# Similarity rows by broadcast DMAs from DRAM, and wider modulations on VectorE from batch 4 on, in a gated cross-attention kernel

## What is computed

```python
def xattn(feature, embedding, weight):              # both (16, 128, 1024), weight (128, 128, 3)
    # per column t: cosine similarity of column t with its left neighbour, itself, its right neighbour
    sim = stack([cos(emb, emb_l), cos(emb, emb), cos(emb, emb_r)], axis=1)   # (16, 3, 1024)
    att = repeat(sim, C, axis=1)                    # (16, 384, 1024): rows 0-127 left, 128-255 own, 256-383 right
    inp_unf = stack([f_pad[:, :, k:k + T] for k in range(3)], axis=2).reshape(B, C * 3, T)
    return einsum('bit,oi->bot', inp_unf * att, weight.reshape(O, C * 3))

def ffn(x):                                         # 8 experts of rank 16, the two best of each token
    gates = top2(softmax(x @ router_w.T + router_b)), normalised
    return einsum('ner,eor->no', (x @ A) * gates, Bm) * 0.5

x = x + tanh(g_xattn) * xattn(layernorm(x), ctx, conv_weight)
x = x + tanh(g_ffn) * ffn(layernorm(x))
```

## Time and profile before

| | |
|---|---|
| median of three runs | 235.19 us (232.73 to 235.48) |
| the profiled execution's own time | 237.36 us |
| its span | 234.8 us |
| TensorE (PE) busy | 216.1 us, 92% |
| VectorE (DVE) busy | 164.7 us, 70% |
| ScalarE (ACT) busy | 112.8 us, 48% |
| GpSimd (POOL) busy | 80.8 us, 34% |
| moved by DMA | 27.24 MB |

### The profile page before, as it was taken

One profiled execution on the slowest core, in us unless ns is written; L12 is line 12 of the kernel. 1 busy time (PEld: TensorE's weight loads), 2 busy tenths in 40 slices (PEclk: granted clock), 3 DMA queues, 4 the chain that ended last, 5 costly groups with the idle time before them and its releaser, 6 DMA issues.

```text
span 234.8 us, 3431 instructions
## 1 busy us (share of the span) xinstructions
PE 216.1 (92%) x1056; PEld 125.5 (53%) x1056; DVE 164.7 (70%) x403; ACT 112.8 (48%) x192; POOL 80.8 (34%) x216
## 2 busy tenths in 40 slices
PE   5878978989999999989999999989999999999954
PEld 5542523636564555547464545546565665666632
DVE  1274986395999666495998665595988777786552
ACT  3566967446387456052577464161647172221210
POOL 2340463205076534032175633032234151412430
PEclk9997999999999999999999999999999999999997
DMA  5789600607022625212233202211142202020132
GB/s 210 267 306 347 264 1 22 248 0 250 20 89 101 259 91 215 100 57 77 89 121 112 93 37 92 89 48 74 59 179 91 91 0 89 3 89 33 57 150 118
DMA packets 8880, 27.24 MB, mean 116 GB/s; under 512 B 1632, under 2 KB 2240, under 8 KB 8864
## 3 DMA queue, kind: packets, MB, share of 16 engines
q1 hardware_dynamic: 8432, 26.78, 30.8%
q10 hardware_dynamic: 432, 0.26, 0.4%
HBM read 18.65 MB, written 8.39 MB: 115 GB/s over the span
## 4 chain that ended last, share of the span: by engine, by line
PE 75%; DVE 13%; issue 4%; POOL 2%; ACT 2%; DMA 2%; POOLq 0%; DVEq 0%
PE bank L852 29%; PE bank L877 13%; PE bank L838 8%; PE bank L804 7%; PE bank L866 5%; DVE pt L661 3%; PE bank L895 3%; PE bank L896 3%; PE bank L897 3%; DVE x L668 2%; DMA et<-ctx 2%; PE bank L824 2%; DVE bn L673 1%; PE bank L902 1%; POOL pr L343 1%
## 5 line engine op out<-in xcount | busy, mean ns | idle before, releaser
L852 PE MATMUL bank<-pt,wT 128*128 128x512 f32 x192 | 99.5, 600 | 0.0
L661 DVE TENSOR_TENSOR pt<-xn,bank 128x512 f32<-128x512 f32 x96 | 63.7, 672 | 12.4 <-PE bank L838 7.9
L877 PEld LDWEIGHTS bank<-aT,xT 128*128 128x128 f32 x256 | 34.4, 190 | 11.1 <-issue 10.2
L838 PE MATMUL bank<-rows,sel 96*128 96x512 bf16 x96 | 36.0, 382 | 3.7 <-DVE pt L661 2.3
L852 PEld LDWEIGHTS bank<-pt,wT 128*128 128x128 f32 x192 | 31.0, 190 | 12.9 <-issue 6.0
L877 PE MATMUL bank<-aT,xT 128*128 128x136 f32 x256 | 34.9, 279 | 0.0
L490 ACT ACTIVATE xT<-bank 128x512 f32<-128x512 f32 x32 | 19.1, 595 | 31.3 <-PE bank L866 31.2
L378 POOL CAST topf<-topi 128x2 f32<-128x2 uint32 x16 | 3.0, 186 | 81.7 <-DVE topi L692 81.7
L668 DVE TENSOR_TENSOR x<-bank,xt 128x512 f32<-128x512 f32 x32 | 21.9, 686 | 9.8 <-PE bank L852 9.8
L705 DVE TENSOR_TENSOR x<-bank,x 128x512 f32<-128x512 f32 x32 | 21.7, 679 | 8.3 <-PE bank L897 8.3
L838 PEld LDWEIGHTS bank<-rows,sel 96*128 96x128 bf16 x96 | 9.2, 97 | 32.8 <-DVE pt L661 16.6
(11 more groups left out here) (86 smaller groups left out, 260.6 us busy)
## 6 DMA issues: line engine op xcount, KB each, us to landing
et<-ctx SPq DMA_DIRECT2D x16, 512.0 KB, 5.8
xt<-x SPq DMA_DIRECT2D x16, 512.0 KB, 3.4
out<-x SPq DMA_DIRECT2D x15, 512.0 KB, 2.6
aT_in<-expert_aT SPq DMA_DIRECT2D x1, 544.0 KB, 13.1
bm_in<-expert_b SPq DMA_DIRECT2D x1, 512.0 KB, 12.3
out<-x SPq DMA_DIRECT2D x2, 256.0 KB, 2.0
sel<-select SPq DMA_DIRECT2D x1, 216.0 KB, 13.5
wT_in<-conv_wT SPq DMA_DIRECT2D x1, 192.0 KB, 6.0
```

The lines of the kernel that those rows point to most:

```text
L661: nc.vector.tensor_tensor(pt[:, i, :], xn[:, n % 2, h * HALF + t:(h + 1) * HALF + t], sim_ps[k % 2][:, :], ALU.mult).then_inc(mod_done, 1)
L838: nc.tensor.matmul(sim_ps[k % 2][:, :], sel[:, SLOT_OF[n], t, :], rows[:, q % 2, half(h)], start=True, stop=True).then_inc(spread, 1)
L852: nc.tensor.matmul(conv_ps[h][:, :], wT[:, t * P:(t + 1) * P], pt[:, i, :], start=(t == 0), stop=(t == TAPS - 1)).then_inc(tap_done, 1)
L877: last = nc.tensor.matmul(h_ps[:, 0:ER + E], xT[:, n % 2, c, :], aT[:, c, :], start=(c == 0), stop=(c == KC - 1))
```

## The change

- From batch 4 on (`SPREAD = 4`) TensorE does not spread similarity rows. The similarities stay fp32 (`simf`), four transposes turn them into rows, ACT copies these to SBUF (`rows_out`), SP stores them to a DRAM tensor `simd` and waits for it (`store_rows`), and loads them back as a tile `att` of 128 partitions x 3 taps x 1024 columns (`load_att`), seven DMAs per batch, into one of three buffers: three DMAs of 42 partitions whose source repeats one row of 4 KB, and four short ones for the two channels whose taps fall into two thirds.
- From batch 4 on VectorE modulates 1024 columns at once from SBUF (`modulate_both`), in the odd steps of the batch before. `pt` has two buffers.
- POOL keeps the products of tiles 1 and 2; all others are VectorE's. POOL sums A's eight blocks into one (`sum_means`), so TensorE's means are one matmul.
- The tables of steps move for groups 2 to 4; `normalize` is issued a step earlier; four more warm-up matmuls; the start's loads are reordered: the two gates first on ACT's queue, the three constants to SP's.
- Code that is not run before or after (for `WHOLE` shorter than six steps) is removed.

```diff
-WARM_UP = 7
+WARM_UP = 11
+SPREAD = 4
-NEIGHBOURS = {(0, 4): 1, (2, 3): 2, (6, 3): 3, (10, 3): 4}
-ROWS = {(0, 5): 1, (3, 0): 2, (7, 0): 3, (11, 0): 4}
-ON_POOL = (1, 2, 5, 7, 9, 11, 13, 15)
+NEIGHBOURS = {(0, 4): 1, (2, 0): 2, (6, 0): 3, (10, 0): 4}
+ROWS = {(0, 5): 1, (2, 1): 2, (6, 2): 3, (10, 2): 4}
+ON_POOL = (1, 2)
...
+            def store_rows(q):
+                sp.wait_ge(rowsf_done, q - 1)
+                for z in range(2):
+                    sp.dma_start(simd[GROUPS[q][0]:GROUPS[q][0] + G, :, PAD + z * HALF:PAD + (z + 1) * HALF].rearrange("b f t -> f b t"),
+                                 rowsf[32 * z:32 * z + 2 * G, :]).then_inc(rows_stored, 16)
+
+            def load_att(n):
+                third = [simd[n:n + 1, 0, PAD - 1:PAD - 1 + T], simd[n:n + 1, 1, PAD:PAD + T], simd[n:n + 1, 0, PAD:PAD + T]]
+                full = P // TAPS
+                j = n % 3
+                sp.wait_ge(rows_stored, 16 + 32 * (GROUP_OF[n] - 1))
+                if n - 3 >= SPREAD:
+                    sp.wait_ge(mod_done, modulations(n - 3))
+                for f in range(TAPS):
+                    c = f * (full + 1)
+                    sp.dma_start(att[c:c + full, j, :, :],
+                                 third[f].unsqueeze(1).to_broadcast([full, TAPS, T])).then_inc(att_in[j], 16)
+                for c in (full, 2 * full + 1):
+                    for f in sorted({(TAPS * c + t) // P for t in range(TAPS)}):
+                        taps = [t for t in range(TAPS) if (TAPS * c + t) // P == f]
+                        sp.dma_start(att[c:c + 1, j, taps[0]:taps[-1] + 1, :],
+                                     third[f].unsqueeze(1).to_broadcast([1, len(taps), T])).then_inc(att_in[j], 16)
...
                 for e in {1: (8, 9), 2: (10, 11), 4: (12, 13), 5: (14, 15)}.get(n, ()):
                     load_e(e)
+                if n % 4 == 2 and n + 2 < B:
+                    store_rows(GROUP_OF[n + 2])
+                if SPREAD <= n + 2 < B:
+                    load_att(n + 2)
...
+            def sum_means():
+                pool.wait_ge(aT_in_done, 16)
+                nc.gpsimd.tensor_tensor(aT_sum[:, :, :], aT_in[:, 0:4, :], aT_in[:, 4:8, :], ALU.add).then_inc(summed_means, 1)
...
+            def rows_out(q):
+                act.wait_ge(rowsT_done, q + 1)
+                if q > 2:
+                    act.wait_ge(rows_stored, 16 + 32 * (q - 2))
+                nc.scalar.activation(rowsf[:, :], rows_ps(q)[0:40, :], ACT.Copy).then_inc(rowsf_done, 1)
...
+            def modulate_both(n, t):
+                dve.wait_ge(xn_done, n + 1)
+                dve.wait_ge(att_in[n % 3], 16 * 7 * (len(range(n % 3, n + 1, 3)) - len(range(n % 3, SPREAD, 3))))
+                dve.wait_ge(tap_done, STEPS * (n - 1))
+                nc.vector.tensor_tensor(pt[:, n % 2, t, :], xn[:, n % 2, t:t + T], att[:, n % 3, t, :],
+                                        ALU.mult).then_inc(mod_done, 1)
...
+                    if SPREAD <= n + 1 < B and i % 2 == 1:
+                        modulate_both(n + 1, i // 2)
+                        some(norms, 2)
...
-            act.dma_start(onehot[:, :, :], one_hot).then_inc(onehot_in, 16)
-            act.dma_start(ident[:, :], identity).then_inc(ident_in, 16)
-            act.dma_start(shifts[:, :, :], shift).then_inc(shifts_in, 16)
+            act.dma_start(gates_in[:, 0:1], g_xattn.rearrange("(a n) -> a n", a=1).to_broadcast([P, 1])).then_inc(gates_in_done, 16)
+            act.dma_start(gates_in[:, 1:2], g_ffn.rearrange("(a n) -> a n", a=1).to_broadcast([P, 1])).then_inc(gates_in_done, 16)
```

More of the change, by code:

```diff
@@ L95, in flamingo_kernel @@
         rows = sb("rows", [96, 2, T], BF16)
+        simf = sb("simf", [P, 4, 2, 32])
+        rowsf = sb("rowsf", [40, HALF])
+        nothing = sb("nothing", [B, PAD])
+        att = sb("att", [P, 3, TAPS, T])
+        simd = nc.dram_tensor("simd", (B, 2, PAD + T), F32).ap()
         xt = sb("xt", [P, G, T])
@@ L159, in rows_ps @@
         def rows_ps(q):
[L160 removed]
+            return sum_ps(q)[:, :].bitcast(BF16) if q < 2 else sum_ps(q)[:, :]
         onehot_in = sem("onehot_in")
@@ L200, in flamingo_kernel @@
         rowsT_done = sem("rowsT_done")
+        rowsf_done = sem("rowsf_done")
+        rows_stored = sem("rows_stored")
+        att_in = [sem(f"att_in{j}") for j in range(3)]
         rows_left_done = sem("rows_left_done")
@@ L239, in flamingo_kernel, with modulations @@
         block = st.enter_context(nc.Block())
-        SETUP = 11
+        SETUP = 13
         def half(h):
             return slice(h * HALF, (h + 1) * HALF)
[L245 to L250, removed]
+        def modulations(n):
+            return STEPS * min(n + 1, SPREAD) + TAPS * max(n + 1 - SPREAD, 0)
         def products_up_to(e):
@@ L537, in _ @@
                     m = STEPS * n + i
-                    for q in (ROWS.get((n, i)),):
-                        if q is not None:
-                            rows_left(q)
-                    for k in steps_at(m, modulated):
-                        if not whole(k):
-                            modulated_hi(k)
+                    if (n, i) in ROWS:
+                        q = ROWS[n, i]
+                        rows_left(q) if q < 2 else rows_out(q)
                     if i == 0 and n >= 2:
                         second_weight(n - 2)
-                    if i == 1 and n + 1 < B:
+                    if i == 0 and n + 1 < B:
                         normalize(n + 1)
@@ L821, in transpose_similarities @@
             def transpose_similarities(q):
+                if q >= 2:
+                    pe.wait_ge(sim_done, q + 1)
+                    for w in range(4):
+                        last = nc.tensor.transpose(rows_ps(q)[0:40, w * P:(w + 1) * P],
+                                                   simf[:, w, :, :].rearrange("p z k -> p (z k)")[:, 0:40], ident[:, :])
+                    last.then_inc(rowsT_done, 1)
+                    return
                 pe.wait_ge(split, 5 * (q + 1))
```

125 lines of the change are left out of this document (57 added, 68 removed).

## The result

The changed kernel takes **273.5 us** (median of four runs, 272.76 to 275.76) against 235.09 us for the kernel before in the same session: 1.166 times as long, 95% interval 1.157 to 1.176. The forecast was 221.8 us.

What follows compares the result with a forecast made beforehand. TensorE, busy 92% of the span, was taken as the bound. -15.8 (spreads) - 2.0 (head) - 1.0 (batch 2) + 5.4 (waits) = -13.4 us, from 237.36 to 224.0, or 221.8 from the 235.19 median; range 213 to 239.

Steps and rivals of the forecast that it cites:

- the rate of the load: Loading att from DRAM: taken as fast as the load of x, 370 GB/s, thanks to equally long 4 KB packets.
- the gap in which it was to hide: Batches without the three waits: att lands after 8.7 us, asked for 9.39 us later at the soonest, hidden by 0.7.
- Rival (3): att loads: reading one 4 KB row from all engines runs at half rate, making the kernel slower, 251 us; chance 0.14.
- decision point: Rival (3): 13.4 us are lost at a load some 2.3 us longer, near 240 GB/s.
- The rule of the Trainium skill on 14 engines: att loads: 42 partitions run on 14 engines, thirds take 4.8 instead of 4.2 us, the sum 1.8 us more.
- The spreads, -15.8: TensorE from batch 4 on: 72 spreads of 0.22 us leave the chain, saving 15.8 us; plain batch 9.39.
- VectorE, 0 but for batch 3: VectorE's modulations gain only evenness; plain batch 8.1 us, hidden behind TensorE's 9.39; batch 3 is 1.1 us late.
- The three waits, +5.4: VectorE waits 2.0 us for att at batches 3, 7 and 11; price 2.6, 1.3 and 1.5, 5.4 us given back.
- The head, -2.0: Start: the gate loads come first on ACT's queue, POOL is free 2.3 us earlier; 2.0 us taken as saved.
- the means cost nothing: Start: experts' means go from 16 TensorE passes (1.86 us) to two, VectorE gets product(5); counted as nothing.
- Batch 2, -1.0: Batch 2: splits into bf16 parts and the copy of rows go; 1.0 of 1.33 us idle TensorE saved.
- the sum: The forecast's terms added up: -13.4 us against the profiled execution's 237.36, giving 224.0, or 221.8 by medians.

Runs made afterwards that it cites:

- sixteen: Changed kernel with each batch's att in three loads of 48, 48 and 32 neighbouring partitions and no short loads: 253.61 us, ratio 1.080.
- after: The changed kernel itself, with 42-partition loads and short pieces, against the kernel before: 273.5 us, ratio 1.166.
- no_short: Changed kernel with att in three loads of 42, 42 and 44 neighbouring partitions and no short loads: 268.46 us, ratio 1.140.
- fast_head: Changed kernel with one 128-partition load per batch from 128 context rows, means on TensorE, products 5 and 7 on POOL: 232.41 us, ratio 0.988.
- wide_distinct: Changed kernel with one load of 128 partitions per batch, from 128 different context rows each read for three taps: 238.21 us.
- wide_same: Changed kernel with one load of 128 partitions per batch, from one repeated row: 244.49 us, ratio 1.038.
- distinct: Changed kernel with the large loads reading another context row for every partition and tap instead of one repeated row: 274.63 us, ratio 1.168.
- gates_first: Kernel before with only the start's loads reordered as in the changed kernel: 235.63 us, ratio 1.0015.
- spread32: Changed kernel with att in four loads of 32 partitions, each taking every fourth partition, from one repeated row: 245.42 us, ratio 1.045.
- noload2: Changed kernel loading att only for batches 4, 5 and 6, later batches using old data: 245.49 us, ratio 1.042.
- warm: Changed kernel with means on TensorE and 70 idle matmuls before experts_out in batches 5, 7 and 11: 286.41 us, ratio 1.220.
- warm32: Changed kernel with means on TensorE and 32 idle matmuls before experts_out in batches 7 and 11: 268.55 us, ratio 1.145.

## Why the prediction was wrong, step by step

**The step that failed** is the rate of the load: "I take it as fast as the load of x, since the packets are as long (4 KB)". I had 6.3 us for a batch's load; with nothing ahead of it in the queue it took 13.4, and in the wide form 7.3 to 8.2. Long packets were not enough: bands of neighbouring partitions (1.9 to 2.9 us of it) made it so, and 14 engines in place of 16 together with the short pieces (some 2.9 from sixteen to after; no run has 42 three times without the short pieces, so these two stay unseparated, and the 2.5 from no_short to sixteen hold the 11 engines that its last band has by the rule above). The repeated row, the only reason against it that I weighed, costs 0.9, and only in a wide load. A load is longer than the gap in which it was to hide, 9.39 us, so eight of the twelve are waited for and not three. The distance of 51.7 us between forecast and result, by medians in order:

| from | to | us |
|---|---|---|
| forecast 221.8 | fast_head 232.4 | 10.6 |
| fast_head | wide_distinct (means by POOL, products 5 and 7 on VectorE) | 5.8 |
| wide_distinct | wide_same (repeated row) | 6.3 |
| wide_same | sixteen (three bands of neighbours) | 9.1 |
| sixteen | no_short (42/42/44) | 14.9 |
| no_short | after (short pieces) | 5.0 |

The causes are not independent, so another order would give other shares; the chips differ too (234.5 to 235.5 us for the kernel before). The load's four lines are together 35.3 us of the 51.7, and 2.7 of these stand in batch 0 of the profiles (45.70 against 43.02 us), which loads no `att`.

**Rival (3)** had the right side and the right rate, half, some 180 GB/s; its decision point, 240 GB/s, was passed. So its sign and rate were right by luck, and not by its reason. Its cause was wrong (distinct), and so was its price, 251 us: it had losses of about 3 us in five batches and 6 in three, where batches 3, 7 and 11 lost 10 to 11 us each and batch 5 lost 5 (after against before). I gave it 0.14 against the argument that the packets are long, which says nothing here. The rule of the Trainium skill on 14 engines stood in the prediction at 1.8 us; from sixteen to no_short, which has 11 engines in its last band by that rule, the count was worth up to 12 (15 less the 2.7 of batch 0), because the load was already longer than its cover.

**The spreads, -15.8**: right. A plain batch is 9.53 us (9.39 forecast).

**VectorE, 0 but for batch 3**: right. Modulations of 1024 columns last 1.20 us (L707), the busy time of a plain batch is 8.18 us (8.1), and with two products in batch 7 of fast_head 10.27 (10.35).

**The three waits, +5.4**: with the wide load, right in place and in their sum (6.9 us for 6.0), though batch 3's is 0.8 and the two others 3. Too small in price. The span of fast_head is 5.1 us shorter than before's and not 13.4, and of these 8.3 us batches 6 and 7 together hold 2.4 (23.5 against 21.1 by the sum) and batches 10 and 11 2.5; batches 0 to 3 hold 3.9 and the rest about nothing. In batch 7 VectorE's wait of 3.1 leaves TensorE idle for 2.6, so hardly any of it was covered; in batch 11 3.0 leave it idle for 2.5, and the slower taps come on top.

**The head, -2.0**: right at its place, lost behind it. Product(2) begins at 13.69 us on POOL (near 13 forecast), the first tap at 20.55 against 22.79 before. The chain of after then reads:

```profile
22.46 0.57 POOL rs L388
...
23.29 1.30 POOL aT_sum L424
...
25.50 1.34 POOL aT_sum L428
26.89 0.82 PE bank L953 x2
27.71 1.71 PE bank L910 x2
```

The product and the tap came sooner as forecast, but the means matmul waits 4.7 us for POOL, whose sums stand behind `feature_rstd(1)`: here "the means cost nothing" fails. I priced what TensorE saves and not what is queued on POOL. Means on TensorE end batch 0 at 39.9 us instead of 45.7; products 5 and 7 on POOL as well, at 38.3. And in gates_first the sooner first tap is worth nothing by the end of batch 1, as the lower clock takes it back.

**Batch 2, -1.0**: right where TensorE has its full clock. Windows of batch 2 in wide_same and in fast_head:

```profile
57.32:67.75 10.43, 10.29 (x52) 6.54 (x52) 7.53 (x19) 5.16 (x12) 3.29 (x12) 1.00 0.62 223
...
52.38:64.48 12.10, 11.96 (x52) 7.39 (x52) 7.56 (x19) 5.15 (x12) 3.27 (x12) 0.86 0.65 241
```

It takes 10.4 us against 11.58 before, also in spread32, noload2, warm and warm32; in after, fast_head and the other kernels built on the changed one it takes 12.1 or more, with the same work, at a granted clock of 0.86 in after and fast_head. So in fast_head batches 1 and 2 together took 26.2 us, 1.6 above the sum.

## What to carry to other kernels

A transfer moved off an engine has to be priced in its own form: how many partitions one DMA covers, whether they are neighbours, and how many DMAs share the work, since here the same 1.5 MB took from 7.3 to 13.4 us; that packets are long says nothing. When a load is to hide in a gap of 9.4 us and the estimate is 8.7, take twice the load as a main case, and not as a rival of 0.14. Work that is put on an idle engine is priced by what stands in its queue in front of the one who waits.

## What the runs showed of the hardware that was not expected

- Loads of 4 KB packets into 32, 42 or 48 neighbouring partitions ran mostly at 100 to 260 GB/s; into every third or fourth partition near 330 in their first microseconds, with a stretch near 200 behind. Bands of 32 ran at half of what the load of x into all 128 reached, 200 against 410 to 437. Why is open: bands of 48 went through a slower stretch (137) than bands of 32 (9.7 us for the whole against 10.5), so both the nearness of partitions and the number for each engine may play a part. Which partitions a band holds was not varied by itself.
- A load of 42 partitions by itself had 14 or 15 packets under way at a time, one of 48 or 32 had 16 or 17.
- A source row that is read again and again cost nothing in the slow form (distinct, 1.168 against 1.166) and 0.9 us of 8.2 in the wide one.
- TensorE's granted clock fell to the lower of its levels behind the long waits (taps of 1.71 instead of 0.86 us), but in fast_head only behind the one in batch 11, of 3.0 us, and not behind the one in batch 7, of 3.1. It also fell where no load is waited for, in batches 0 and 2. It was worth some 2 us a time, and held up in warm32 it brought nothing.
